# Two of four attention stages computed by key tiles instead of by query tiles

## The reference, cut to what matters

```
idx_s = jnp.argmax(route[:, :K], axis=-1)
xn = _ln(x, norm_s_w, norm_s_b)
# spatial: weights of expert idx_s
q = q.reshape(B, T, H, HD) * HD ** (-0.5)
att = jax.nn.softmax(jnp.einsum('bthd,bshd->bhts', q, k), axis=-1)
o = jnp.einsum('bhts,bshd->bthd', att, v).reshape(B, T, D)
...
# cross: queries from the spatial output, keys and values from the temporal output
fused = _cross_mha(spatial_out, temporal_out, cross_in_w, cross_in_b, cross_out_w, cross_out_b)
```

## Time and profile before

| | |
|---|---|
| median of 3 runs | 3285.45 us (3285.14 to 3288.96) |
| profiled execution: time, span | 3288.95 us, 3287.2 us |
| granted clock, mean | 0.947 |
| busy: PE, DVE, ACT, POOL | 89%, 61%, 46%, 29% of the span |

### The profile page before, as it was taken

How to read it: one execution, slowest core, us unless ns; L and a number is a source line. 1 busy time by engine, 2 the same in 40 slices (tenths; PEclk the granted TensorE clock), 3 DMA queues, 4 the chain that set the end, 5 groups by cost and what they waited for, 6 DMA issues and landing times. The chain is left out here.

```text
span 3287.2 us, 48200 instructions
## 1 busy us (share of the span) xinstructions
PE 2928.7 (89%) x15718; PEld 2072.6 (63%) x15718; DVE 1999.0 (61%) x4063; ACT 1519.8 (46%) x3320; POOL 944.6 (29%) x994
## 2 busy tenths in 40 slices
PE   5978699999589958699998888989999899998899
PEld 3622287776467635355555865668777687776787
DVE  6888736776421126699995355643777537776444
ACT  3500035666035426477774345533666336664322
POOL 2067564670134430677770000000000000001210
PEclk9999999999689979799998998999999999999999
DMA  3067664331569953545541544136320163311322
GB/s 100 13 173 206 189 162 117 61 75 41 168 194 339 340 170 141 200 148 151 155 115 35 189 120 104 25 107 184 71 59 22 51 190 82 64 25 40 108 80 84
DMA packets 222612, 402.75 MB, mean 123 GB/s; under 512 B 44222, under 2 KB 140626, under 8 KB 218526
## 3 DMA queue, kind: packets, MB, share of 16 engines
q1 hardware_dynamic: 170866, 262.09, 28.1%
q0 software_dynamic: 49744, 134.92, 14.8%
q10 hardware_dynamic: 1756, 2.64, 0.3%
HBM read 315.84 MB, written 87.71 MB: 123 GB/s over the span
## 5 line engine op out<-in xcount | busy, mean ns | idle before, releaser
L904 ACT ACTIVATE at_p<-at_pb,at_max 125x1250 f32<-125x1250 f32 (+4 forms) x320 | 383.8, 1199 | 301.5 <-DVE at_unused L975 272.6
L790 PE MATMUL at_pb<-ident,at_p 125*125 125x125 f32 x2880 | 436.0, 282 | 18.7 <-ACT at_p L904 15.8
L790 PEld LDWEIGHTS at_pb<-ident,at_p 125*125 125x125 f32 x2880 | 393.1, 192 | 82.2 <-ACT at_p L904 21.4
L807 PE MATMUL at_pb<-at_pt,at_v 125*64 125x250 f32 x2880 | 356.6, 384 | 5.2 <-DVE s_t L1008 3.0
L968 DVE TENSOR_REDUCE at_wide<-at_pb 125x1 f32<-125x1024 f32 x240 | 293.6, 1223 | 21.7 <-PE at_pb L773 3.4
L890 ACT ACTIVATE at_pt<-at_pb 125x500 f32<-125x500 f32 (+1 forms) x448 | 232.8, 520 | 99.2 <-PE at_pb L790 95.2
L807 PEld LDWEIGHTS at_pb<-at_pt,at_v 125*64 125x64 f32 x2880 | 188.6, 137 | 104.2 <-issue 14.9
L750 PE MATMUL at_pb<-at_s,at_shared 128*128 128x500 f32 (+1 forms) x1152 | 230.1, 362 | 23.7 <-ACT at_shared L852 23.7
L986 DVE COPY at_pt<-at_pb 125x500 f32<-125x500 f32 (+1 forms) x416 | 232.1, 582 | 21.6 <-PE at_pb L790 21.6
L975 DVE TENSOR_SCALAR_CACHE_REDUCE at_unused<-at_pb,at_wide 125x226 bf16<-125x226 f32 x240 | 107.7, 449 | 204.8 <-PE at_pb L773 201.9
L750 PEld LDWEIGHTS at_pb<-at_s,at_shared 128*128 128x128 f32 x1152 | 196.4, 194 | 56.9 <-ACT at_shared L852 24.4
(11 more groups left out here) (337 smaller groups left out, 5693.7 us busy)
## 6 DMA issues: line engine op xcount, KB each, us to landing
w_ring<-in_L_ffn_w SPq DMA_DIRECT2D x128, 512.0 KB, 11.5
at_shared<-k_parts SPq DMA_DIRECT2D x64, 312.5 KB
ml_w<-in_mlp_w SPq DMA_DIRECT2D x64, 256.0 KB
k_parts<-at_shared SPq DMA_DIRECT2D x64, 250.0 KB, 2.8
q_parts<-at_shared SPq DMA_DIRECT2D x64, 250.0 KB, 3.0
h_edges<-em_both SPq DMA_DIRECT2D x11, 1024.0 KB, 4.3
g_h<-h_edges SPq DMA_DIRECT2D x11, 1024.0 KB, 6.2
at_shared<-q_parts SPq DMA_DIRECT2D x32, 312.5 KB
```

The lines of the kernel that those rows point to most:

```text
L790: ins = pe.transpose(pturn[0:TN, g % 2, TN * (t % 4):TN * (t % 4) + TN], p[:, u % 2, TN * t:TN * t + TN], c.ident[0:TN, 0:TN])
L807: ins = pe.matmul(pout[side:side + 64, 0:2 * TN], v[:, t, 2 * j + h, :], p_t[:, q % 2, t, :], start=(t < 2), stop=(t >= keys[u] - 2))
L904: act.activation(p[:, t % 2, 0:w], score[t % 2][0:TN, 0:w], ACT.Exp, bias=neg_max[:, t:t + 1], accum_out=total[:, t:t + 1]).then_inc(exp_d ...
```

## The change

The spatial and the cross attention call a new function, `attention_by_key`. It does the following.

- The scores are computed transposed: 125 keys on the partitions, queries along the columns. The result of exp then has the layout that the multiplication with v needs, so the transposes and their copies are gone, as are the adds of two halves.
- A pass is one head times half of the queries (2 x 312 or 2 x 316 columns, with 6 columns twice): 16 passes (`PASSES`) of 10 steps, one step for each tile of keys. Two steps are a double step: there are 80 (`DUOS`).
- The maximum of each query must now be known before its scores are computed. It comes from a coarse product of high parts only (`max_piece`, 3 pieces of 418, 416 and 416 columns for 125 queries, 240 pieces in all), reduced on DVE, negated, and written by SP with five DMAs of 125 values into row 64 of `qb` (`neg` to `MAXROW`); the second score matmul has 65 rows, and the row of ones in `kb` adds the negative maximum. The pieces of a pass run 8 to 4 double steps ahead of it (`LEAD = 8`). The first scores of a pass wait for `row_in`.
- The row sums are sums over keys, now across tiles: DVE adds four times in a pass and POOL four times (125x624 or 125x632 values), and PE sums the two results over the partitions with a matmul with ones (`sums`). For 13 passes ACT copies the sum and sends it through two small DMAs to DVE, which inverts it, and POOL multiplies some passes later. For the last three (`DIRECT`) DVE inverts 64 copies of it in PSUM and multiplies the output itself (`scale_now`).
- The projection's order is q, k, v; SP loads the first pair back in the midst of it (two groups of 6 loads), not POOL. The 24 pieces of the first pass and part of the second stand between the tiles of v.

The core of the diff; `for P in range(PASSES)` with `sp.` is SP's queue, `max_piece(u, m)` with `pe.`, `scores`, `values` and `sums` are PE's, and the last loop is DVE's.

```diff
@@ -1020,6 +1020,610 @@
+QUARTERS = ((0, 312), (618, 316))
+MAX_CUTS = ((0, 418), (418, 834), (834, N))
+def attention_by_key(nc, c, q_src, kv_src, out_t, wq_d, wk_d, wv_d, bq_d, bk_d, scratch, pick=None, send=None,
+                     save=None, early=None, after=None, ahead=False, columns=None):
...
+        for P in range(PASSES):
+            for k in range(15):
+                pieces_at[NT // 2 * P - LEAD + k // 3].append((P, k // 3, k % 3))
+        sums_at = {NT // 2 * (P + 1) + 1: P for P in range(PASSES)}
...
+                for P in range(PASSES):
+                    j, h, half = P // 4, P // 2 % 2, P % 2
+                    sp.wait_ge(max_ready, P + 1)
+                    for i in range(5):
+                        a = 625 * half + TN * i
+                        sp.dma_start(qb[j % 2][h][MAXROW, a:a + TN].bitcast(F32).rearrange("o (p i) -> o p i", p=TN),
+                                     neg[:, P, i:i + 1].bitcast(F32)).then_inc(row_in, 16)
+                    if P % 4 == 0:
+                        if j + 1 < PAIRS_:
+                            if j == 0:
+                                sp.wait_ge(summed, NI)
+                            else:
+                                sp.wait_ge(scored, 4 * NT * j)
+                            load_pair(sp, j + 1, "qk", kq_in[(j + 1) % 2])
...
+                def max_piece(u, m):
...
+                    slot_free(k)
+                    pe.matmul(bank[0:TN, 4 + k % 2, 0:b - a], qa[j % 2][h][:, q0:q0 + TN], ka[j % 2][h][:, a:b],
+                              start=True, stop=True).then_inc(filled, 1)
...
+                    if kind == "v":
+                        if x == first_v:
+                            pe.wait_ge(first_in, 16 * LOADS)
...
+                def scores(s):
...
+                    if t == 0:
+                        pe.wait_ge(row_in, 80 * (P + 1))
...
+                    if s >= 2:
...
+                        pe.wait_ge(exp_done, s - 1)
+                    keys = slice(TN * t, TN * t + TN)
+                    at = lambda x: bank[0:TN, 2 * ((s + 1) % 2) + x, 0:wide(half)]
+                    for x in range(2):
+                        pe.matmul(at(x), ka[j % 2][h][:, keys], qa[j % 2][h][:, slice(*chunk(half, x))], start=True, stop=False)
+                    for x in range(2):
+                        ins = pe.matmul(at(x), kb[j % 2][h][0:65, keys], qb[j % 2][h][0:65, slice(*chunk(half, x))],
+                                        start=False, stop=True)
...
+                def values(s):
...
+                    for x in range(2):
+                        ins = pe.matmul(bank[64 * x:64 * x + 64, 6 + P % 2, 0:wide(half)], v[:, t, 2 * j + h, :],
+                                        p[:, s % DEEP, x, 0:wide(half)], start=(t == 0), stop=(t == NT - 1))
...
+                def sums(P):
...
+                    pe.wait_ge(dve_added, len(by_dve) * (P + 1))
+                    pe.wait_ge(pool_added, len(by_pool) * (P + 1))
+                    for g in range(2):
+                        for x in range(2):
+                            ins = pe.matmul(bank[64 * x:64 * x + 64, 4 + k % 2, 0:w], ones[:, :], acc[:, P % 2, g, x, 0:w],
+                                            start=(g == 0), stop=(g == 1))
...
+                for u in range(DUOS + 2):
+                    for m in range(2):
+                        max_piece(u, m)
+                        if u < DUOS:
+                            scores(2 * u + m)
+                    max_piece(u, 2)
+                    if 1 <= u <= DUOS:
+                        values(2 * u - 2)
+                        values(2 * u - 1)
+                    if u in sums_at:
+                        sums(sums_at[u])
...
+                for u in range(DUOS + 2):
+                    max_piece(u, 0)
+                    if 1 <= u <= DUOS:
+                        add(2 * u - 2)
+                    max_piece(u, 1)
+                    max_piece(u, 2)
+                    if 1 <= u <= DUOS:
+                        add(2 * u - 1)
@@ -2512,17 +3116,17 @@
-                attention(nc, c, s_t, s_t, s_t, whalf(sw, 0), whalf(sw, 1), whalf(sw, 2), bcol(sbr, 0), bcol(sbr, 1), scratch,
+                attention_by_key(nc, c, s_t, s_t, s_t, whalf(sw, 0), whalf(sw, 1), whalf(sw, 2), bcol(sbr, 0), bcol(sbr, 1), scratch,
...
-                attention(nc, c, s_t, t_t, s_t, zero(whalf(cw, 0)), zero(whalf(cw, 1)), zero(whalf(cw, 2)),
+                attention_by_key(nc, c, s_t, t_t, s_t, zero(whalf(cw, 0)), zero(whalf(cw, 1)), zero(whalf(cw, 2)),
```

More of the change, by code:

```diff
@@ L2514, in program @@
                           early=all_w(a["tp_w"]), columns=(bcol(a["tv_bcol"]), all_b(a["tp_b"])), after=lambda wo: out_features(
-                              nc, c, t_t, wo, load_first(c, whalf(sw, 1), (bcol(sbr, 0), bcol(sbr, 1)), spatial), residual_d=t_d))
-                attention(nc, c, s_t, s_t, s_t, whalf(sw, 0), whalf(sw, 1), whalf(sw, 2), bcol(sbr, 0), bcol(sbr, 1), scratch,
+                              nc, c, t_t, wo, load_first(c, whalf(sw, 0), (bcol(sbr, 0), bcol(sbr, 1)), spatial), residual_d=t_d))
+                attention_by_key(nc, c, s_t, s_t, s_t, whalf(sw, 0), whalf(sw, 1), whalf(sw, 2), bcol(sbr, 0), bcol(sbr, 1), scratch,
                           pick=spatial, early=all_w(a["sp_out_w"]), ahead=True, columns=(bcol(sbr, 2), all_b(a["sp_out_b"])),
                           after=lambda wo: out_features(nc, c, s_t, wo, load_first(
-                              c, zero(whalf(cw, 1)), (zerob(bcol(cbr, 0)), zerob(bcol(cbr, 1))))))
+                              c, zero(whalf(cw, 0)), (zerob(bcol(cbr, 0)), zerob(bcol(cbr, 1))))))
                 def out1(wo):
```

470 lines of the change are left out of this document (added).

## The result

The changed kernel takes 3300.58 us (median of five, 3297.66 to 3306.93), the kernel before beside it 3286.07: a ratio of 1.0047, 95% interval 1.0034 to 1.0061. It is slower by 15 us, where 12.5 us less had been forecast. The profiled execution took 3297.66 us.

The account below looks back on a forecast made before the run. The prediction took PE's starts to bound the loop: -37.3 us saved, +6 for the first pair's loads and +18.8 for rows of maxima made -12.5, from 3285.45 to 3273 us; range 3246 to 3295, the forecast's own 3262 to 3284.

Parts of the forecast that it names:

- The new loop's price on PE: Both main loops: 3.215 us per double step, 277.0 us per loop, saving 17.6 us in spatial and 19.7 in cross.
- first_in: After the first v tile PE waits for the first pair's loads: 3 us in each stage, 6 us together.
- POOL and DVE fit beside PE: Main loop: DVE needs 14.5 us of a 17.1 us pass, with POOL adding at the same time.
- The rows' waits of the spatial loop: PE waits for maxima behind the 12 loads: 6.0 us at pass 1, 1.7 each at passes 5 and 9, together 9.4.
- DVE's additions: Main loop: an addition of 624 or 632 values takes 0.82 us alone, 1.27 assumed with POOL adding too.
- the price of the 24 pieces: Maximum pieces between the v tiles, counted in PE's loop work at PE's own 0.192 us per 417 columns.
- it fits: ACT in the main loop: two exp of about 0.8 us per 3.2 us, two copies, five DMA issues a pass.
- The first (rows pass the loads): Rival: rows of maxima don't wait behind the loads, or slack hides it; -31.3 us, 3254 us; chance 0.22.
- The second (half clock behind stalls): Rival: each of eight stalls also drops PE's clock, 2.4 us each, 19 us; +6.7, 3292 us, slower; chance 0.15.
- The third: Rival: DVE becomes the loop's bound, needing additions of 1.92 us; at 2.07 us the time is 3292 us; chance 0.06.
- the fourth: Rival: matmuls with 65 rows or changing halves start slower; 0.1 us per double step cancels the gain, 3285 us; chance 0.12.
- seven stalls at 2.4 us: Within the half-clock rival: clock drops at PE's stalls decide the result from 7 stalls on, at 2.4 us each.

Follow-up runs that it names:

- later_first: The kernel both with every group of maximum pieces one v tile later, the first inside the third v tile; 3237.87 us, ratio 0.9860 to before.
- late_sums: Changed kernel with ACT issuing the two transfers of a pass's sums behind step 8 instead of step 3; 3313.06 us, ratio 1.0072 to before.
- spread_v: Changed kernel with the three maximum pieces behind a v tile put inside the next v tile; 3286.42 us, ratio 0.9993 to before.
- both: spread_v plus the 12 loads issued in two lots of 6, at the eighth steps of a pair's first two passes; 3254.09 us, ratio 0.9899 to before.
- late_loads: Changed kernel with the 12 loads in one lot behind the row transfers of the pair's second pass, not its first; 3295.08 us, ratio 1.0022.

## Why the prediction was wrong

**What was right.** The new loop's price on PE: a double step was measured at 3.10 to 3.18 us against 3.215, one with sums at 4.2 against 4.2. Undisturbed, the loop takes 268.1 us (later_first) where the prediction has 277.0 less the 4.6 for the 24 pieces outside it, 272.4. So the saving was larger than forecast by 4.3 us in the spatial and 4.5 in the cross stage. `first_in`, 2.4 and 2.9 against 3. POOL and DVE fit beside PE, and the place of the rows' waits was right.

**Where a number was right by luck.** The rows' waits of the spatial loop, 9.2 against 9.4 us, are two misses that cancel. The row lands 21.6 to 21.9 us after the first load, the prediction had 20.6, so pass 1 waits 7.2 and not 6.0; passes 5 and 9 wait 1.2 and 0.8 and not 1.7 because ACT's stall had held PE up before; without that stall they wait 3.9 and 3.8 (late_sums). And DVE's additions, 1.24 to 1.30 in the mean (L1575) against 1.27, are a mixture: 0.80 us each when POOL did nothing beside, 1.47 to 1.50 with an addition of POOL's over most of it. The contention is larger than assumed, and falls on about half of them.

**The step that failed** is the price of the 24 pieces that stand between the tiles of v. They were counted at 0.192 us each, PE's own time, "with the 24 pieces that stand between the tiles of v" in one half-sentence, without asking who frees their two PSUM slots. In the loop, scores and products lie between the pieces, and DVE's reduction is hidden; between the tiles they stand in a row, and each group waits for DVE. Forecast for the stretch, 28.6 + 4.6 + 3.0 = 36.2 us; measured 46.2 and 48.0. That is 10.0 and 11.8 us, 21.8 of the 27.6 that separate 3273 from 3300.6; 7.1 of the 10.0 are the spatial stage's waits for DVE. spread_v shows 17 of them to be the order of the pieces; later_first shows the rest to be `first_in` with the half clock behind: without both the stretch is 4.4 and 6.0 us shorter than in the kernel both, against the 3.0 forecast for each.

**Steps that were off in size**, in the spatial loop: forecast 272.4 + 9.4 = 281.8, measured 284.4 (284.0 in cross). The undisturbed loop is 4.3 us less, the waits for rows 0.2 less; 4.1 us are the new waits for ACT, and the rest, 3.0 us, is what 6.1 us of PE's work at half clock behind the longest wait cost. The prediction said of ACT "it fits", by counting its busy time, and took the issue of a transfer as cheap even behind a burst of loads. That ACT's stall is a loss by itself, as I thought after the first trace, was wrong, as late_sums showed: passes 5 and 9 were to be late by the rows anyway. The sum of stall and row wait there (3.0 and 3.2 us) stands against a forecast of 1.7 each.

**The rivals.** The first (rows pass the loads) fell: they pass them neither in SP's queue nor beside another. The second (half clock behind stalls) holds in part. In the changed kernel it happened around the two waits of 7.2 us, those for `first_in` (2.44, 2.85) and those of 1.87 and 2.16 us for ACT in the cross loop, not behind those of 1.74 and 2.36 us in the spatial one, nor behind any of 0.8 to 1.2; what decides it between 1.7 and 2.4 us is not shown. It is worth at most 3.6 us in the spatial loop and 5.4 in the cross loop (PE's busy time against later_first), so it alone would not have turned the sign. (Nor do seven stalls at 2.4 us, as the prediction says, reach the 3292 from which a result is slower: they end at 3290.) The third and the fourth fell.

## What to carry to other kernels

When work is moved to a place where it stands in a row, its price is no longer its own engine's: ask which slots it needs, who frees them and what that engine waits for first; the same piece cost 0.19 us between scores and 0.59 in a row. When a burst of large loads is issued, look at every small transfer that starts in its time, on whichever queue, and place the burst, in lots, where it is over before the next of them matters; here that was worth 30 us and cost nothing. And two waits behind one cause don't add: take away the cause, since taking one of them away leaves their sum as it was or makes it longer (at passes 5 and 9, 6.1 us became 6.5 in late_loads and 7.7 in late_sums).

## What the hardware showed

- The issue of a transfer can hold its engine while a burst of loads is under way. ACT's two issues took 1.3 to 1.8 us in quiet times, 3.9 to 4.3 at 9.2 us after a burst of 3.84 MB began, 5.0 to 5.8 at 15.0 us; five of SP's 3.5 to 3.8 in quiet times, 6.1 to 7.2 right behind the loads. It was so too when the loads were in GpSimd's queue (ACT 4.1 to 4.6, SP 5.3 to 8.6). Full DMA engines alone do not do it: in late_loads ACT's two took 1.78 us and SP's five 3.80, 12 to 14 us into a burst with the engines' share at 1.04. What does is open.
- A row of 625 tiny packets landed 20.5 to 22.3 us after the first of 12 loads was issued, wherever PE waited for one, whether the loads were in its own queue or in GpSimd's.
- An addition of 125x624 float32 values on DVE took 0.80 us alone and 1.47 to 1.50 us with an addition of POOL's beside it.
- In the kernels with the new loop PE's granted clock was 0.50 for 3.4 to 10 us around every wait of 2.5 us and more, around some of those between 1.7 and 2.5 us, and around none of 0.8 to 1.3. In the kernel before it stayed at 1.00 behind a wait of 3.17 us.
